# Macaron block on one core: attention stacks sent in two parts, k projection spread over the steps, causal mask of the first pass added by TensorE

## What is computed

```python
x = x + 0.5 * moe(layernorm(x), gate, up, down, topk_idx, topk_weight)
x = x + attn(layernorm(x), Wqkv, b_qkv, Wout, b_out)
x = x + 0.5 * moe(layernorm(x), gate, up, down, topk_idx, topk_weight)

def attn(x, Wqkv, b_qkv, Wout, b_out):        # 16 heads of 32, S = 512
    q, k, v = split(x @ Wqkv.T + b_qkv)
    scores = einsum('bqhd,bkhd->bhqk', q, k) * scale + alibi_bias   # bias depends on the key alone
    scores = where(causal, scores, -1e9)
    return einsum('bhqk,bkhd->bqhd', softmax(scores), v) @ Wout.T + b_out
```

## Time and profile before

| | |
|---|---|
| median of 3 runs | 3004.56 us |
| profiled execution | 3000.08 us, of which its span is 2998.4 us |
| granted TensorE clock, mean | 0.938 of full |
| TensorE matmul busy | 2562.4 us (85%), 13156 instructions |
| VectorE busy | 1534.4 us (51%) |
| ScalarE busy | 1375.9 us (46%) |
| attention, 1118 to 2126 us of the span | TensorE busy 903.3 of 1008 us, granted clock 0.89 to 0.92 |

### The profile page before, as it was taken

The page is one execution under the profiler, slowest core; times in us unless marked ns, Lnnn a source line. Parts: engine busy times, 40 slices in busy tenths (PEclk is TensorE's granted clock), DMA queues, the critical chain, the costliest instruction groups (busy, mean ns, idle before and its releaser), DMA issues. The chain is left out here.

```text
span 2998.4 us, 67154 instructions
## 1 busy us (share of the span) xinstructions
PE 2562.4 (85%) x13156; PEld 1885.8 (63%) x13157; DVE 1534.4 (51%) x3734; ACT 1375.9 (46%) x3572; POOL 1099.5 (37%) x913
## 2 busy tenths in 40 slices
PE   0229999999999378989989898998599999999994
PEld 0117888888888245555555555555378888888883
DVE  8764554555543336564564646455345555555431
ACT  0216666666655323232232323232166666666652
POOL 3434655565555200001011010101245655555552
PEclk9999999999999778998989888898799999999997
DMA  5436877888854423232332323333167787888545
GB/s 154 134 125 156 189 179 179 188 186 185 193 94 53 100 57 79 78 76 74 92 85 77 80 71 78 85 78 86 60 170 179 187 189 170 189 192 197 96 55 144
DMA packets 155637, 377.83 MB, mean 126 GB/s; under 512 B 33277, under 2 KB 34685, under 8 KB 155298
## 3 DMA queue, kind: packets, MB, share of 16 engines
q0 software_dynamic: 76416, 168.58, 29.0%
q1 hardware_dynamic: 68256, 198.28, 23.1%
q10 hardware_dynamic: 10882, 10.14, 1.1%
HBM read 236.63 MB, written 126.88 MB: 121 GB/s over the span
## 5 line engine op out<-in xcount | busy, mean ns | idle before, releaser
L504 POOL DMA_INDIRECT x_rows<-f_ob,f_it x320 | 514.3, 1607 | 573.3 <-ACT f_ob L651 240.0
L554 PE MATMUL f_psg<-f_wh,f_xh 128*128 x1280 | 535.4, 418 | 4.7 <-DVE f_xl L722 4.7
L554 PE MATMUL f_psg<-f_wh,f_xl 128*128 x1280 | 504.9, 394 | 0.0
L554 PE MATMUL f_psg<-f_wl,f_xh 128*128 x1280 | 502.1, 392 | 0.0
L496 POOL DMA_INDIRECT f_xg<-xn_rows,f_it x320 | 356.4, 1114 | 112.6 <-issue 94.5
L1309 DVE CUSTOM_DVE_ANT_0 a_psa<-a_psa,cst 128x128 f32<-128x128 f32 (+3 forms) x512 | 249.8, 504 | 189.2 <-PE a_psa L1096 186.6
L1225 ACT ACTIVATE a_pt<-a_psb 128x256 f32<-128x256 f32 (+3 forms) x512 | 213.3, 438 | 284.4 <-PE a_psb L1144 279.6
L1017 POOL CAST a_cth<-a_ct 128x512 fp32r<-128x512 f32 x32 | 19.6, 612 | 798.5 <-DVE a_ct L1333 798.5
L651 ACT ACTIVATE f_ob<-f_pso,f_wcol 128x512 f32<-128x512 f32 x320 | 220.7, 690 | 192.5 <-issue 116.1
L1096 PE MATMUL a_psa<-a_stk,a_stq 98*128 98x128 f32 (+3 forms) x512 | 230.5, 458 | 79.0 <-DVE a_mx L1309 41.9
L722 DVE TENSOR_TENSOR f_xl<-f_psx,f_xh 128x512 fp32r<-128x512 f32 x320 | 221.4, 692 | 137.3 <-ACT f_xh L632 90.7
(11 more groups left out here) (186 smaller groups left out, 4383.6 us busy)
## 6 DMA issues: line engine op xcount, KB each, us to landing
f_wraw<-w_in SPq DMA_DIRECT2D x128, 768.0 KB
a_stq<-a_qk SPq DMA_DIRECT2D x128, 192.0 KB
a_stk<-a_qk SPq DMA_DIRECT2D x128, 192.0 KB
r_xt<-x_in SPq DMA_DIRECT2D x32, 256.0 KB, 4.4
xn_rows<-r_xo SPq DMA_DIRECT2D x32, 256.0 KB, 2.9
a_xt<-x_rows SPq DMA_DIRECT2D x8, 1024.0 KB, 5.2
a_x<-x_rows SPq DMA_DIRECT2D x8, 1024.0 KB, 5.5
x_rows<-a_x POOLq DMA_DIRECT2D x8, 1024.0 KB, 5.0
```

The costliest lines, as they stand in the source:

```text
L504: g.indirect_dma_start(x_d, bass.IndirectOffsetOnAxis(it[:, n:n + 1], 0), ob[:, n % OB, :], None, compute_op=ALU.add).then_inc(s_sca[n % O ...
L554: mm = pe.matmul(psg[:, j, :], x[:, j, k, :], w[:, cols], start=(k == 0 and n == 0), stop=(k == DC - 1 and n == 2))
```

## The change

- `stacks`: each unit's DMAs are sent in two parts. Part one takes columns 0 to 383 of every row (eight DMAs of 96 rows and two for the bias, semaphore `s_stk`) once the second pass of unit u has made 12 of its 16 products; part two takes columns 384 to 511, again ten DMAs, on a semaphore of its own (`s_stl`), once it has made all 16. A unit has 20 stack DMAs.
- First pass: its products run tile by tile (t the slow index), are spread over steps 0 to 12 (two at each of steps 0 to 2, table `A_AT`), and each is followed by a bf16 product of 128 columns that adds the causal mask in PSUM. Tiles 0 to 2 need part one alone, tile 3 waits for part two. VectorE takes `tensor_reduce` with max.
- k projection: its four chunks stand behind steps 0, 1, 3 and 5. Only the q projection is ahead of the steps.
- ScalarE's high q stands behind exponential 1, high k behind exponential 7; both wait for `s_stk` and `s_stl`. VectorE's low q stands behind maximum 4, low k behind maximum 11; statistics, row normalisation and row low parts of the next batch are spread over the maxima, and the row turns over steps 9, 10, 12 and 14.
- `turn_maxima` stands behind step 15, ahead of the last contexts; in g = 3 the values come after it, and `normalise` always after `negated`.

```diff
-    X_AT = {8: 0, 10: 1, 14: 2}
+    LATE = S - P
+    A_AT = {0: (0, 1), 1: (2, 3), 2: (4, 5), 3: (6,), 4: (7,), 5: (8,), 6: (9,), 7: (10,), 8: (11,), 9: (12,),
+            10: (13,), 11: (14,), 12: (15,)}
+    K_AT = {0: 0, 1: 1, 3: 2, 5: 3}
+    X_AT = {9: 0, 10: 1, 12: 2, 14: 3}
+    STATS_AT = {5: (0,), 7: (1,), 9: (2,), 12: (3, TB)}
+    ROW_AT, LOW_AT = {5: 0, 6: 1, 8: 2, 9: 3}, {12: 0, 13: 1, 14: 2, 15: 3}
...
+            if not (last and g == 3):
+                found += [("m", g)]
             if g == 3 and not last:
                 found += [("v", t) for t in range(TB)]
-            if not (last and g == 3):
-                found += [("m", g)]
...
-                    if not below(u, 2):
-                        sp.wait_ge(s_b, u * 16 - 16)
-                    for j in range(HG):
-                        rows = slice(j * HD, (j + 1) * HD)
-                        for n, to in enumerate((stq, stk)):
-                            sp.dma_start(raw(to[0:3 * HD, slot + j, :]), raw(qk3[rows, n, :, :])).then_inc(s_stk, 16)
-                    for r in range(2):
-                        sp.dma_start(raw(stk[3 * HD + r:3 * HD + r + 1, slot:slot + HG, :]),
-                                     raw(bias_r[g4 * HG:(g4 + 1) * HG, r, :])).then_inc(s_stk, 16)
+                    for done, cols, told in ((12, slice(0, LATE), s_stk), (16, slice(LATE, S), s_stl)):
+                        if not below(u, 2):
+                            sp.wait_ge(s_b, u * 16 - (32 - done))
+                        for j in range(HG):
+                            rows = slice(j * HD, (j + 1) * HD)
+                            for n, to in enumerate((stq, stk)):
+                                sp.dma_start(raw(to[0:3 * HD, slot + j, cols]), raw(qk3[rows, n, :, cols])
+                                             ).then_inc(told, 16)
+                        for r in range(2):
+                            sp.dma_start(raw(stk[3 * HD + r:3 * HD + r + 1, slot:slot + HG, cols]),
+                                         raw(bias_r[g4 * HG:(g4 + 1) * HG, r, cols])).then_inc(told, 16)
...
-                def scores_row(u, slot, j, *tiles):
-
-                    h = slot * HG + j
-                    for t in tiles:
-                        n = j * TB + t
-                        if not (below(u, 1) and n < 2):
-                            pe.wait_ge(s_am, u * 16 + (n - 1))
-                        out = psa[:, t % 2, 0:(t + 1) * P]
-                        pe.matmul(out, stq[0:3 * HD + 2, h, t * P:(t + 1) * P], stk[0:3 * HD + 2, h, 0:(t + 1) * P],
-                                  start=True, stop=True).then_inc(s_a, 1)
+                def scores_row(u, slot, *tiles):
+
+                    for i in tiles:
+                        t, h = i // HG, slot * HG + i % HG
+                        if i == 0:
+                            pe.wait_ge(s_stk, u * STK + STK)
+                        if t == TB - 1 and i % HG == 0:
+                            pe.wait_ge(s_stl, u * STK + STK)
+                        if not (below(u, 1) and i < 2):
+                            pe.wait_ge(s_am, u * 16 + (i - 1))
+                        pe.matmul(psa[:, i % 2, 0:(t + 1) * P], stq[0:3 * HD + 2, h, t * P:(t + 1) * P],
+                                  stk[0:3 * HD + 2, h, 0:(t + 1) * P], start=True, stop=False)
+                        pe.matmul(psa[:, i % 2, t * P:(t + 1) * P], masks[:, 0, :], causal[:, S - P:S],
+                                  start=False, stop=True).then_inc(s_a, 1)
...
-                def attention(bk, b, g, a_on, x_on):
+                def attention(bk, b, g, p_on, a_on, x_on):
 
                     u = b * NG + g
+                    if p_on:
+                        out = take(bk, "q", g)
+                        if g == 2:
+                            pe.wait_ge(s_wfd, bk.read("x", TB - 1)[1])
+                        project(out, (g + 2) % NG, 0, range(DC)).then_inc(s_w, 1)
                     pe.wait_ge(s_mr, u * 32 + 32)
                     if g == 0:
...
+                            if a_on and n in A_AT:
+                                scores_row(u + 1, (g + 1) % 2, *A_AT[n])
                             if kt and j % 2:
                                 context(u, g, kt - 1, j // 2)
-                            if a_on:
-                                if n == 0:
-                                    pe.wait_ge(s_stk, u * STK + 2 * STK)
-                                scores_row(u + 1, (g + 1) % 2, n // TB, n % TB)
+                            if p_on and n in K_AT:
+                                k = K_AT[n]
+                                if k == 0:
+                                    out = take(bk, "k", g)
+                                mm = project(out, (g + 2) % NG, 1, (k,))
+                                if k == DC - 1:
+                                    mm.then_inc(s_w, 1)
                             if x_on and n in X_AT:
                                 turn_x(bk, b + 1, X_AT[n])
-                    if x_on:
-                        turn_x(bk, b + 1, TB - 1)
+                            if a_on and n == 15:
+                                turn_maxima(bk, u + 1, g, (g + 1) % 2)
...
                     for g in range(NG):
-                        u = b * NG + g
-                        if not (last and g >= 2):
-                            for n, name in enumerate("qk"):
-                                out = take(bk, name, g)
-                                if g == 2 and n == 0:
-                                    pe.wait_ge(s_wfd, bk.read("x", TB - 1)[1])
-                                project(out, (g + 2) % NG, n, range(DC)).then_inc(s_w, 1)
-                        a_on = not (last and g == 3)
-                        attention(bk, b, g, a_on, g == 1 and not last)
-                        if a_on:
-                            if g == 3:
-                                values(bk, range(TB))
-                            turn_maxima(bk, u + 1, g, (g + 1) % 2)
+                        attention(bk, b, g, not (last and g >= 2), not (last and g == 3), g == 1 and not last)
+                    if not last:
+                        values(bk, range(TB))
                     output(bk, b)
...
                         a.wait_ge(s_stk, u * STK)
+                        a.wait_ge(s_stl, u * STK)
                     a.activation(qk3[:, n, 0:2 + n:1 + n, :],
...
+                def probability(u, n):
+                    kt, j = n // HG, n % HG
...
-                        for kt in range(TB):
-                            if kt < 2 and not (last and g >= 2):
-                                high(bk, u + 2, g, (g + 2) % NG, kt)
-                            probabilities(u, kt)
-                            if g == 1 and kt >= 2 and not last:
-                                rows_high(bk, b + 1, range(kt * 2 - 4, kt * 2 - 2))
-                        if g == 3 and not last:
-                            values(bk)
+                        for n in range(HG * TB):
+                            probability(u, n)
+                            if n in (1, 7) and not (last and g >= 2):
+                                high(bk, u + 2, g, (g + 2) % NG, n // 7)
+                            if g == 1 and n in X_AT and not last:
+                                rows_high(bk, b + 1, (X_AT[n],))
                         if not (last and g == 3):
                             maxima(u + 1, (g + 1) % 2)
+                    if not last:
+                        values(bk)
...
+                def maximum(u, slot, i):
+                    t, j = i // HG, i % HG
+                    at = j * TB + t
+                    v.wait_ge(s_a, u * 16 + (i + 1))
+                    v.sem_inc(s_spare_v, 1)
+                    v.tensor_reduce(mx[:, slot, at:at + 1], psa[:, i % 2, 0:(t + 1) * P], AX.X,
+                                    ALU.max).then_inc(s_am, 1)
...
+                        for i in range(HG * TB):
+                            if not (last and g == 3):
+                                maximum(u + 1, (g + 1) % 2, i)
+                            if i in (4, 11) and not (last and g >= 2):
+                                low(bk, u + 2, g, (g + 2) % NG, i // 11)
+                            if g == 0 and i in STATS_AT and not last:
+                                means(b + 1, *STATS_AT[i])
+                            if g == 1 and i in ROW_AT and not last:
+                                row(bk, b + 1, ROW_AT[i])
+                            if g == 1 and i in LOW_AT and not last:
+                                row_low(bk, b + 1, LOW_AT[i])
                         if not (last and g == 3):
                             negated(bk, u + 1, g)
-                        if g < 3:
-                            normalise(u)
+                        normalise(u)
```

(45 more changed lines are left out.)

32 lines of the change are left out of this document (6 added, 26 removed).

## The result

The change makes the kernel slightly slower: 3012.95 us (median; 3010.18 to 3021.47) against 3004.92 us (3000.88 to 3010.76) for the kernel before in the same sessions. The ratio is 1.0034, interval 1.0026 to 1.0042. The forecast was 3050 us: the sign was right, the size was not. The spans of the profiled executions are 3011.3 and 2998.4 us; they lie 4.9 us further apart than the medians.

What follows compares the result with a forecast made beforehand. TensorE runs nearly without a pause in attention; after the change, part two's landing gates g = 1 to 3: +8.1 us, g = 0 -1.7, so +6.4 a batch, +45 over 7 batches, last batch 0: 3050 us, range 2955 to 3105.

Steps and rivals of the forecast that it cites:

- The queue of SyncE: SyncE's 20 stack DMAs a unit take 0.685 us an issue, 13.7 us; the last lands 15.3 us after step 11's mask.
- rival A: SyncE issues small DMAs in 0.4 us, TensorE's work binds: 2960 us, or 2925 with the clock up; chance 0.16.
- rival B: SyncE takes 0.58 us an issue, the point where the sign turns: 3004 us, within 6; chance 0.09.
- The gate and the pause: High q waits for part two ahead of exponential 2, so TensorE waits 3.5 us ahead of step 4.
- t15: Start of step 15's mask product on TensorE, taken as the beat; forecast 3.0 us after t11.
- t11: Start of step 11's mask product on TensorE; SyncE's first part-one DMA was forecast 0.26 us after it.
- Steps 4 to 15: TensorE from step 4 to step 11's mask: 7.7 us at full clock, then 3.0 us to step 15.
- The mask product: Each added mask product in TensorE's first pass costs 0.02 us, bounds -0.05 and +0.23; 0.1 us for seven.
- The half clock: After the waits in g = 1 to 3 TensorE's clock falls as in g = 3, costing 3.4 us more a period.
- rival C: Gate holds but half clock costs 1.6, not 3.4 us: 3012, or 2985 with quicker issue; chance 0.08 for below 2998.
- g = 0: First unit of a batch, stacks long landed: the wait for statistics goes, 26.3 us become 24.6, 1.7 less.
- The last batch: A gated unit (+3 us) and two unit starts without a projection, helped by the earlier turn (-3): 0.

Runs made afterwards that it cites:

- high q late: Changed kernel with ScalarE's high q behind exponential 5 in place of 1 and VectorE's low q behind maximum 7 in place of 4: 2912.17 us, ratio 0.9694.
- three pairs of kernels: With and without mask products: changed (3012.95 us) and mask by VectorE (3020.23); before (3004.92) and before plus mask (3018.45); high q behind exponential 5 (2912.17) and mask by VectorE (2903.75).
- k ahead and high q late in g = 0: Changed kernel with high q behind exponential 5 and, in g = 0 alone, the k projection ahead of the steps: 2911.81 us, ratio 0.9698.

## Why the prediction had the sign and not the size

**The queue of SyncE: right.** The forecast had 20 issues of 0.685 us, landing 15.3 us behind step 11. They took 0.66, and high q went at 1437.90 where step 11 had its mask at 1423.35: 14.55 us. The rows show 0.58 to 0.63 us of queue for 144 KB as for 48 KB, which at the rate of the earlier trace rows, 192 KB in about 1.0 us, would need 0.75 and 0.25 us (estimates). The Trainium skill's rule (DMA: Bandwidth & Descriptors, "Issuing engines are not separate DMA queues") that initiating a DMA is usually small beside the DMA is not borne out by them. With 0.66 us an issue rival A (0.4 us) falls, and rival B (0.58 us) too.

**The gate and the pause: right in kind, short by a third.** TensorE was forecast at step 4's door 10.4 us behind t15; it was there at 10.4 (1437.61 - 1427.23) and 10.9 in g = 3. Forecast was the opening at 13.9; it came at 12.3 and 13.3. The pause is 1.9 to 2.5 us in place of 3.5: from the quicker queue and landing (0.75 us), and for g = 2 also from a later t15, as in g = 1 ahead of it row turns stand between steps 11 and 15 (t15 is 3.88 us behind t11, not 3.0). Two terms ahead of the door were off and cancelled: the wait for the maxima's rows was 0.15 and 0.75 us and not 1.5, and steps 0 to 4 take 5.2 us from mask to mask without a gate, where about 4.6 were taken.

**Steps 4 to 15: too short, and hidden by the gate.** 7.7 us at full clock were forecast from the start of step 4 to the mask of step 11, and 3.0 from there to step 15. With high q late, at full clock, they take 8.15 and 3.10 in g = 2 and 3. In the changed kernel, with the time at half clock counted half, they take 8.4 and 3.10. Over the three beats the steps are some 2.8 us longer than forecast, row turns included, while step 4 opens 3.3 us sooner. The two errors cancel, which is luck.

**The mask product: mis-sized.** Forecast 0.02 us with an upper bound of 0.23, measured 0.08 to 0.10, from the work of three pairs of kernels. I had read that a mask hides a weight load of the product behind it. These rows of the changed kernel show the time turning up again:

```profile
1447.02 0.42 PE L1106 MATMUL a_psa<-a_stk,a_stq 98*128 98x384 f32 x1
1447.29 0.23 PE L1108 MATMUL a_psa<-cst,a_masks 128*128 128x128 bf16 x1
1447.33 0.36 PE L1159 MATMUL a_psb<-a_stq,a_stk 100*128 100x256 f32 x1
1447.53 0.23 PE L1161 MATMUL a_psb<-a_masks 128*128 128x128 bf16 x1
```

The first-pass product of 384 columns holds TensorE for 0.27 us, as before, with a mask behind it, and the 256 columns of the second pass, which held it for 0.12 us before (1448.02 to 1448.14), now hold it for 0.20. Nothing was hidden; that the time is the weight load is my reading, no row shows it. Seven of a unit's sixteen masks stand at steps 0 to 3 and fill the pause; the nine behind them are, at 0.08 us too little each, most of the error in steps 4 to 15.

**The half clock: the step that failed.** "The clock will fall as in g = 3, 3.4 us more" was taken for each of three units. In the middle batches the stretches at half in g = 1 to 3 of the changed kernel are 3.4, 3.4 and 4.0 us long on average, costing half: 5.4 us a batch and not 10.2. At full clock the forecast of the three beats is 85.0 - 10.2 = 74.8, the measured one 79.8 - 5.4 = 74.4. So nearly the whole miss of the three beats, 4.8 of 5.2 us, is this term once the two errors above have cancelled, and over seven batches it is 34 of the 37 us between the forecast and the median. The earlier trace rows hold both sorts of stretch, in g = 2 and in g = 3 (6.8 us; the one of g = 2 adds up to 3.4 us, the clock at 0.56 and 0.73 in its end windows, and not to the 3.2 of the forecast), and I took the longer one for every unit because a wait of nearly 2 us had stood ahead of it. The other middle batches of the kernel before say the same (g = 3: 6.8 us in five of six), yet waits of 1.9 to 2.5 us in the changed kernel have 3.4 us behind them in 17 of 18 units. So the length of the pause alone doesn't tell the stretch, and a term that the rows show at two values should have been carried at both, with about even chances. The lower one was rival C, priced at 3012 us; its chance of 0.08 stood for results below 2998 alone, and 3012 us itself was the lower edge of the forecast's own 0.55. That 3012 was met within 1 us is partly luck, since the terms below cancel too.

**g = 0:** forecast 1.7 us less, measured 2.6 less. Pauses fall by 2.8 us, among them the wait of 2.6 us behind the statistics, and the half clock gives back 1.3, against 1.4 us more work. TensorE still has one long wait there,

```profile
1381.63 0.33 PE L1106 MATMUL a_psa<-a_stk,a_stq 98*128 98x128 f32 x1 [2.06 <-DVE a_mx L1323]
```

with 6.8 us at half behind it.

**The last batch:** forecast 0, measured +6.3, of it 4.9 in g = 0. In the kernel before it has no statistics to wait for and runs from the first mask to the last in 12.8 us at full clock, its k projection covering VectorE's output tail:

```profile
2046.07 0.44 PE L1096 MATMUL a_psa<-a_stk,a_stq 98*128 98x384 f32 x1 [0.55 <-DVE a_mx L1309]
```

In the changed kernel the k chunks stand behind the first-pass product that waits,

```profile
2047.13 0.33 PE L1106 MATMUL a_psa<-a_stk,a_stq 98*128 98x128 f32 x1 [2.05 <-DVE a_mx L1323]
...
2048.00:2052.00 4.00, 4.00 (x15) 2.67 (x14) 2.01 (x5) 1.20 (x2) 0.61 (x2) 0.51 0.97 353
```

and the unit takes 21.4 us: it starts 3.7 us sooner behind the beat and loses 8.6. I had priced the earlier turn there and not what the moved k projection had covered. With k ahead and high q late in g = 0, the last batch is 4.2 us shorter.

Together: 45 us forecast, less 7 x 4.8 for the clock, less 7 x 0.9 for g = 0, plus 6.3 for the last batch, gives 11, where the profiles show 9.4 in attention. The measured +8 us lies well inside the range; the direction, 0.66 for slower, was right.

## What to carry to other kernels

When a transfer is split so that readers can start on its first part, look for everyone who waits for the whole: here an overwrite of the source kept its place ahead of work on the critical path, and moving that wait two exponentials down, from behind 1 to behind 3, took 104 us off, where the change with the wait in its first place had lost 8. A wait in an engine's program holds all that stands behind it, so it belongs where its event has already happened. And price a pause of TensorE with the clock behind it from many instances of the same pattern, not from one.

## What the runs showed of the hardware

- In the changed kernel an issue from SyncE of a DMA within SBUF takes 0.58 to 0.65 us of its queue, 0.66 from issue to issue, for 48 KB as for 144 KB; a third of the size takes no less of the queue. Loads of x from HBM took 0.38 us in the same queue.
- In the middle batches of the changed kernel and of the one with high q late, stretches at the lower clock were 3.4 or 6.8 us long, behind pauses of about 2 us; with the k projection ahead some were 10 to 27 us long. After the wait for VectorE in g = 0 of the kernel with high q late (1.99 to 2.05 us) none followed in two of six middle batches, 3.4 us in one and 6.8 us in three. What decides is open.
- A bf16 mask product of 128 columns added to an fp32 product costs TensorE 0.08 to 0.10 us a piece over a batch (estimates from the work of three pairs of kernels), though the next one starts 0.04 us behind it.
- The plain maximum is hardly quicker for VectorE than mask and maximum in one, over 512 columns 0.688 against 0.699 us; what goes is the reading of the accumulator, 0.141 us each. The Trainium skill (VectorE: DVE Perf Modes, "Rules for kernel authors") calls `tensor_reduce` the slowest operation; here it is no slower than what it replaces.

```profile
L1323 DVE TENSOR_REDUCE a_mx<-a_psa 128x1 f32<-128x512 f32 x124 | 83.3, 688 | 20.4 <-PE a_psa L1108 20.0
...
L1321 DVE CUSTOM_DVE_ANT_0 a_psa<-a_psa,cst 128x512 f32<-128x512 f32 x121 | 83.9, 699 | 12.0 <-PE a_psa L1106 10.2
L1321 DVE DVE_READ_ACCUMULATOR2_ANT a_mx<- 128x1 f32 x493 | 69.6, 141 | 0.0
```
